# A Mamba block with attention and experts on one core: odd token tiles of the state sum move from VectorE to ScalarE and GpSimd

## What is computed

```python
def step(s, inp):
    d_t, B_t, C_t, u_t = inp
    dA = jnp.exp(d_t[..., None] * A)
    dBu = d_t[..., None] * B_t[:, None, :] * u_t[..., None]
    s = s * dA + dBu
    y = jnp.einsum('bds,bs->bd', s, C_t)     # sum over the 16 states
    return (s, y)
```

## Time and profile before

| what | value |
| --- | --- |
| time, median of 3 runs | 1225.23 us (1220.23 to 1236.71) |
| profiled execution, first to last instruction | 1224.7 us |
| VectorE busy | 922.6 us (75%) |
| TensorE busy | 929.7 us (76%) |
| GpSimd busy | 528.2 us (43%) |
| ScalarE busy | 489.6 us (40%) |
| state sums on VectorE (lines 1100 and 1103) | 256, of which 240 take 167.3 us |
| scan of chunk 0 | 62.8 to 181.4 us |
| ticks 3 to 20 of the scan of chunk 1 | about 258 to 361 us |

### The profile page before, as it was taken

How to read it: one execution, slowest core, us unless ns; L and a number is a source line. 1 busy time by engine, 2 the same in 40 slices (tenths; PEclk the granted TensorE clock), 3 DMA queues, 4 the chain that set the end, 5 groups by cost and what they waited for, 6 DMA issues and landing times.

```text
span 1224.7 us, 13783 instructions
## 1 busy us (share of the span) xinstructions
PE 929.7 (76%) x3960; PEld 700.9 (57%) x3960; DVE 922.6 (75%) x1323; ACT 489.6 (40%) x911; POOL 528.2 (43%) x311
## 2 busy tenths in 40 slices
PE   4845549668689899577689899486789896677996
PEld 2434435256468685165477785165468683554885
DVE  2699996589999966689999965789789965322233
ACT  3534423544246434454345424454245421211442
POOL 1266540453457740533367730544257741001553
PEclk9855558778669999678679899678579997665999
DMA  5100101201023211101023211201023212000331
GB/s 193 36 35 35 52 1 35 70 35 61 18 70 121 77 45 54 70 35 61 18 78 127 73 36 55 85 18 61 18 72 119 86 35 91 21 1 9 117 109 42
DMA packets 38254, 72.61 MB, mean 59 GB/s; under 512 B 3871, under 2 KB 12712, under 8 KB 38174
## 3 DMA queue, kind: packets, MB, share of 16 engines
q1 hardware_dynamic: 38174, 71.65, 17.8%
HBM read 65.14 MB, written 2.30 MB: 55 GB/s over the span
## 4 chain that ended last, share of the span: by engine, by line
PE 45%; DVE 23%; issue 20%; POOL 6%; ACT 3%; DVEq 1%; POOLq 0%; DMA 0%; ACTq 0%; SPq 0%
PE ps L862 11%; DVE hs L1051 7%; PE ps L939 7%; PE ps L718 6%; PE ps L797 5%; POOL dbu L531 4%; DVE yacc L1103 4%; PE ps L836 3%; PE ps L791 2%; PE ps L825 2%; DVE work L1219 2%; PE ps L881 2%; PE ps L776 2%; DVE xn L1014 1%; POOL work L563 1%
## 5 line engine op out<-in xcount | busy, mean ns | idle before, releaser
L531 POOL TENSOR_TENSOR dbu<-v,bbc 128x1024 f32<-128x1024 f32 x128 | 308.9, 2418 | 257.3 <-DVE hs L1051 136.3
L1051 DVE TENSOR_TENSOR_SCAN hs<-ps,carry,dbu 128x512 f32<-128x512 f32 x256 | 313.3, 1266 | 10.1 <-ACT ps L627 8.2
L627 ACT ACTIVATE ps<-delta,neg_a 128x512 f32<-128x512 f32 x256 | 175.7, 692 | 300.5 <-DVE hs L1051 300.4
L718 PE MATMUL ps<-ident,hs 128*128 128x128 f32 x1024 | 189.1, 344 | 116.5 <-DVE yacc L1103 99.5
L718 PEld LDWEIGHTS ps<-ident,hs 128*128 128x128 f32 x1024 | 157.0, 180 | 150.0 <-DVE hs L1051 72.4
L1103 DVE SCALAR_TENSOR_TENSOR yacc<-ps,ctok,yacc 128x512 f32<-128x512 f32 x240 | 167.3, 737 | 1.2 <-PE ps L718 1.0
L555 POOL TENSOR_TENSOR w_lo<-w13s,w_hi 128x512 fp32r<-128x512 f32 x72 | 94.5, 1313 | 145.1 <-ACT w_hi L693 145.1
L939 PE MATMUL ps<-w2s,work 128*128 128x256 f32 x576 | 140.4, 388 | 0.3
L939 PEld LDWEIGHTS ps<-w2s,work 128*128 128x128 f32 x576 | 109.0, 196 | 15.9 <-DVE work L1225 1.5
L1219 DVE SCALAR_TENSOR_TENSOR work<-work 128x512 f32<-128x512 f32 x72 | 82.3, 1143 | 46.5 <-POOL work L563 45.6
L862 PE MATMUL ps<-x_hi,w_hi 128*128 128x512 f32 x288 | 107.9, 457 | 9.4 <-DVE work L1225 9.2
(11 more groups left out here) (159 smaller groups left out, 1243.0 us busy)
## 6 DMA issues: line engine op xcount, KB each, us to landing
w13s<-in_w SPq DMA_DIRECT2D x72, 256.0 KB, 2.9
bbc<-brow_dram SPq DMA_DIRECT2D x32, 512.0 KB, 4.0
w2s<-in_w SPq DMA_DIRECT2D x36, 256.0 KB, 2.7
cbc<-comb_dram SPq DMA_DIRECT2D x32, 256.0 KB, 3.5
work<-work SPq DMA_DIRECT2D x16, 256.0 KB, 2.3
xn<-in_x SPq DMA_DIRECT2D x5, 512.0 KB, 5.3
xt<-in_x SPq DMA_DIRECT2D x4, 512.0 KB, 3.6
rope<-in_rope_q SPq DMA_DIRECT2D x4, 512.0 KB, 4.2
```

The lines of the kernel that those rows point to most:

```text
L531: pool.tensor_tensor(dbu[:, i % DRING, :, :], v[:, 2 * h:2 * h + 2, :], bbc[:, n // 2 % 2, n % 2, :].rearrange("p (o t) -> p o t", o=1) .t ...
L627: act.activation(ps[:, unit % 2, :], delta[:, q, :], ACT.Exp, scale=neg_a[:, q * NS + m:q * NS + m + 1]).then_inc(da_done.sem, 1)
L718: last = pe.transpose(ps[:, bank, t * P:(t + 1) * P], src(t), ident[:, :])
L1051: dve.tensor_tensor_scan(hs[:, m % 2, q, 0:TC], ps[:, unit % 2, :], dbu[:, n % DRING, q % 2, :], carry[:, m, q:q + 1], ALU.mult, ALU.add). ...
```

## The change

For the first nine states (`SHARE = 9`) the odd token tiles are no longer summed by VectorE. ScalarE multiplies PSUM bank 3 by the column of `ctok` (`weigh`), for state 0 straight into `yacc`, for states 1 to 8 into `weighed`, which is the space of `xt`. GpSimd adds `weighed` to `yacc` (`add_weighed`). Even tiles, and all tiles of states 9 to 15, stay with VectorE. A new step, scan2, stands between scan and late: in it ScalarE weighs and then makes the second of its two decays, and GpSimd adds. The semaphore `y_done` is split into four; the transposes of an odd tile of the first nine states wait for `y_mul`, which ScalarE raises. The load of `xt` goes from the start of a body (pre 3) to tick 31 of the scan, behind the last add.

```diff
@@ schedule
-        steps += [("early", t), ("sum", s), ("mid", t), ("scan", s), ("late", t)]
+        steps += [("early", t), ("sum", s), ("mid", t), ("scan", s), ("scan2", s), ("late", t)]
@@ tiles
+        weighed = xt[:, :, :].rearrange("p (a b) n -> p a (b n)", a=2)
@@ sync
-                if kind == "pre" and n == 3:
-                    sp.wait_ge(*res_done.at(j, 0))
+                if kind == "scan" and n == SCAN_TICKS - 4:
+                    sp.wait_ge(*y_add.at(j, 2 * (SHARE - 1)))
                     sp.dma_start(xt[:, :, :], x[bass.ds(j, 1)].rearrange("a t p d -> p (a t) d")
                                  ).then_inc(xt_in.sem, 16)
@@ gpsimd
+                if kind == "scan2" and 5 <= n < 3 + 2 * SHARE:
+                    add_weighed(j, *divmod(n - 3, 2))
...
+            def add_weighed(j, n, half):
+
+                t = 2 * half + 1
+                pool.wait_ge(*y_mul.at(j, 2 * n + half + 1))
+                pool.wait_ge(*y_add.at(j, max(0, 2 * (n - 2) + half + 1)))
+                pool.tensor_tensor(yacc[:, t, :], yacc[:, t, :], weighed[:, half, :], ALU.add
+                                   ).then_inc(y_add.sem, 1)
@@ scalar
-                if kind == "scan":
-                    for unit in range(2 * n + 2 if n else 0, min(2 * n + 4, NS * Q)):
+                if kind == "scan2" and 3 <= n < 3 + 2 * SHARE:
+                    weigh(j, *divmod(n - 3, 2))
+                if kind in ("scan", "scan2"):
+                    ahead = 2 * n + 2 + (kind == "scan2")
+                    for unit in ([ahead] if n or kind == "scan2" else [0, 1, ahead]):
+                        if unit >= NS * Q:
+                            continue
...
+            def weigh(j, n, half):
+
+                t = 2 * half + 1
+                act.wait_ge(*ht_ps.at(j, n * NT + t + 1))
+                if n == 0:
+                    act.wait_ge(*ctok_done.at(j, 1))
+                    act.wait_ge(*xz_ps.at(j, 2 * Q))
+                    act.activation(yacc[:, t, :], ps[:, 3, :], ACT.Copy, scale=ctok[:, t, n:n + 1]).then_inc(y_mul.sem, 1)
+                else:
+                    if n == 1:
+                        act.wait_ge(*res_done.at(j, 0))
+                    else:
+                        act.wait_ge(*y_add.at(j, 2 * (n - 2) + half + 1))
+                    act.activation(weighed[:, half, :], ps[:, 3, :], ACT.Copy, scale=ctok[:, t, n:n + 1]
+                                   ).then_inc(y_mul.sem, 1)
@@ tensor, state_rows
-                    pe.wait_ge(*y_done.at(j, max(0, n * NT + t - 1)))
+                    before = 2 * n + t // 2
+                    if t % 2 == 0:
+                        pe.wait_ge(*y_even.at(j, before))
+                    elif before <= 2 * SHARE:
+                        pe.wait_ge(*y_mul.at(j, before))
+                    else:
+                        pe.wait_ge(*y_odd.at(j, before - 2 * SHARE))
                     transposes(2 + t % 2, lambda q: hs[:, n % 2, q, t * P:(t + 1) * P], Q, ht_ps)
@@ vector, sum_states
                     c = ctok[:, t, n:n + 1]
+                    if t % 2 and n < SHARE:
+                        continue
```

More of the change, by code:

```diff
@@ L43 @@
 HRING = 3
+SHARE = 9
 DRING = 3
@@ L280, in block_kernel @@
         ht_ps = signal("ht_ps", NS * NT)
-        y_done = signal("y_done", NS * NT)
+        y_even = signal("y_even", 2 * NS)
+        y_odd = signal("y_odd", 2 * (NS - SHARE))
+        y_mul = signal("y_mul", 2 * SHARE)
+        y_add = signal("y_add", 2 * (SHARE - 1))
         yt_ps = signal("yt_ps", Q)
@@ L629, in mixer @@
                     m = n // 2 - 1
-                    if n % 2 == 0 and 0 <= m < NS:
+                    if kind == "scan" and n % 2 == 0 and 0 <= m < NS:
                         act.wait_ge(*scan_done.at(j, Q * (m + 1)))
                         act.activation(carry[:, m, :], hs[:, m % 2, :, TC - 1], ACT.Copy).then_inc(carry_done.sem, 1)
+            def weigh(j, n, half):
[12 more added lines that the diff above has]
+                                   ).then_inc(y_mul.sem, 1)
             def convolution_start(j, q):
@@ L781, in mixer @@
                 if kind == "post" and n == 0:
-                    for t in range(NT):
-                        pe.wait_ge(*y_done.at(j, (NS - 1) * NT + t + 1))
+                    pe.wait_ge(*y_even.at(j, 2 * NS))
+                    pe.wait_ge(*y_odd.at(j, 2 * (NS - SHARE)))
                     for q in range(Q):
@@ L1099, in sum_states @@
                         dve.wait_ge(*xz_ps.at(j, 2 * Q))
-                        dve.tensor_scalar(yacc[:, t, :], ps[:, 2 + t % 2, :], c, None, ALU.mult).then_inc(y_done.sem, 1)
-                    else:
-                        dve.wait_ge(*y_done.at(j, (n - 1) * NT + t + 1))
-                        dve.scalar_tensor_tensor(out=yacc[:, t, :], in0=ps[:, 2 + t % 2, :], scalar=c,
-                                                 in1=yacc[:, t, :], op0=ALU.mult, op1=ALU.add).then_inc(y_done.sem, 1)
+                        dve.tensor_scalar(yacc[:, t, :], ps[:, 2, :], c, None, ALU.mult).then_inc(y_even.sem, 1)
+                    elif t % 2 == 0:
+                        dve.wait_ge(*y_even.at(j, (n - 1) * 2 + t // 2 + 1))
+                        dve.scalar_tensor_tensor(out=yacc[:, t, :], in0=ps[:, 2, :], scalar=c,
+                                                 in1=yacc[:, t, :], op0=ALU.mult, op1=ALU.add).then_inc(y_even.sem, 1)
+                    else:
+                        if n == SHARE:
+                            dve.wait_ge(*y_add.at(j, 2 * (SHARE - 2) + t // 2 + 1))
+                        else:
+                            dve.wait_ge(*y_odd.at(j, (n - 1 - SHARE) * 2 + t // 2 + 1))
+                        dve.scalar_tensor_tensor(out=yacc[:, t, :], in0=ps[:, 3, :], scalar=c,
+                                                 in1=yacc[:, t, :], op0=ALU.mult, op1=ALU.add).then_inc(y_odd.sem, 1)
             def row_stats(j, k, src, t, before):
```

## The result

The changed kernel takes 1279.25 us (median of 4 runs, 1277.19 to 1289.54); the kernel before 1225.44 us (4 runs). The ratio is 1.0407, interval 1.0356 to 1.0458: slower by about 4%. The profiled execution has a span of 1279.3 us against 1224.7.

The account below looks back on a forecast made before the run. VectorE was taken to bound chunk 0 only, a loop through four engines chunks 1 to 3. The sum was 1224.7 - 2 + 3 x 17 = 1273.7 us, said as 1273, with a range of 1211 to 1300.

Parts of the forecast that it names:

- The likeliest case of the four: Chunks 1 to 3: transposes held back by the weighing, as walked; 1273 us, range 1251 to 1294, chance 0.64.
- VectorE is not the bound in chunks 1 to 3: Ticks 3 to 20: VectorE's work stands in a loop round four engines, one turn 10.65 us; VectorE binds chunk 0 only.
- The rival of 1178 us: Whole kernel: VectorE is the bound and all 72 sums, 46.8 us, come off; chance 0.09.
- Prices: Added work: 72 weighings on ScalarE at 0.69 us, 64 adds on GpSimd at 1.26 us, moved xt load zero.
- Bank 3 free 2.7 us after the first scan starts: Each changed tick: scan 1.27, exp 0.69, weighing 0.69 and hand-overs pass before the odd transposes can start.
- The walk through chunk 1: Ticks 3 to 20 followed instruction by instruction: first scans shift from -1.3 us at tick 4 to +17 at tick 21.
- 17 us per chunk: Chunks 1 to 3: loss in each from late transposes and what queues behind them; bounds 10 to 23 us.
- the rival of the falling clock: Chunks 1 to 3: longer gaps may lower TensorE's granted clock to 0.6; 1273 + 24 = 1297 us, chance 0.09.
- The collision of top with a dbu: Tick 5, chunk 1: top runs beside a dbu delayed by an add, takes 1.30 us against 0.17 alone, ends with it.
- Chunk 0: Scan without attention beside it: -2 us (0 to -4), with GpSimd at 3.61 us per tick against 3.67.
- GpSimd allows less: 2.35 + 1.26 = 3.61 per tick: Chunk 0: GpSimd's dbu and add limit the tick, against 3.67 before; 1 us over 16 ticks.
- The hidden case, 1211 us: Whole kernel: the wait hides and only short ticks gain, 11.7 us and 2 in chunk 0; with collisions alone, chance 0.18.

Follow-up runs that it names:

- weigh_at_sum: Changed kernel with ScalarE's weighing moved to the step sum, ahead of the exp that waits for the scan: 1243.32 us, ratio 1.0066 to the kernel before.
- weigh_last: Changed kernel with ScalarE's weighing moved behind both exps of the tick: 1354.91 us in one run, 1.097 times the median of the kernel before.
- no_odd: Changed kernel without the odd sums of the first nine states on any engine, nor the wait for bank 3: 1197.95 us, ratio 0.9745 to the kernel before.
- split_only: Kernel before with only the two exps of a tick split as in the change: 1233.02 us, ratio 1.0031.
- no_add: Changed kernel without GpSimd's 64 adds and the waits for them, weighing kept: 1283.89 us, ratio 1.0403 to the kernel before.
- weigh_first: Changed kernel with the weighing in a step of its own, ahead of everything in the tick: 1229.38 us, ratio 1.0008 to the kernel before.
- same_tick: Changed kernel with each tile weighed one tick earlier, behind its own transposes: 1224.65 us, ratio 0.9975 to the kernel before.
- first_chunk: Kernel before with the change in chunk 0 only, one odd tile in two ticks, weighed first; exps split, xt late: 1220.58 us, ratio 0.9845; again 1221.6, 0.9855.

## Why the prediction was right

**The sum.** 1273 was predicted, 1279.25 measured, the span 1279.3 against 1273.7: 54.6 us more instead of 49. The likeliest case of the four happened, for its reason: weigh_at_sum takes five sixths of the loss away and weigh_last more than doubles it, by the place of one instruction.

**VectorE is not the bound in chunks 1 to 3: right.** no_odd is the direct measure. Without the 72 sums the kernel gains 31 us and not 46.8; chunk 0 gives the whole of its part, the three others about half of theirs in the profile, and less at a like clock. (The shares were read a little high: 95.92 of 107.90 us is 89%, so VectorE was busy for 89 to 95%.) The rival of 1178 us is out of reach even for a kernel that does not do the work at all. The Trainium skill, "Perfetto Trace Analysis", section "Optimizing Scalar/DVE Operations", says that moving work off a saturated DVE may make sense. Here VectorE is saturated in chunk 0 alone, and the ratios are 1.0407 as it was done, 1.0008 with the weighing first and 0.9845 with chunk 0 alone.

**Prices: nearly right.** The weighing took 0.67 us (0.69 taken), the add 1.285 (1.26). Moving the load of xt was not tried alone; at the same clock no stage shows a cost or a gain from it.

**Bank 3 free 2.7 us after the first scan starts: right.** In tick 4 the scan starts at 264.09, the weighing ends at 266.80 and the transposes start at 266.86, after 3.27 us of waiting.

**The walk through chunk 1: right in its steps.** Where the earlier trace rows has the transposes of normalised x 0.06 us behind VectorE's pieces, and 0.14 us behind the start of the scan, tick 16 of the changed kernel has:

```profile
353.93 2.44 DVE L1093 TENSOR_TENSOR_SCAN hs<-ps,carry,dbu 128x512 f32<-128x512 f32 x2
...
355.96 0.67 ACT L667 ACTIVATE xt<-ps,ctok 128x512 f32<-128x512 f32 x1
...
356.68 1.11 PE L754 MATMUL ps<-ident,hs 128*128 128x128 f32 x4 [5.36 <-ACT xt L667]
...
357.59 1.91 PE L754 MATMUL ps<-ident,x 128*128 128x128 f32 x8
```

They start 3.66 us behind the scan (3.8 predicted). The shift of a tick's first scan, in us, each chunk from its own tick 2:

| tick | predicted | chunk 1 | chunk 2 | chunk 3 |
|---|---|---|---|---|
| 4 | -1.3 | -0.2 | 0.0 | -1.0 |
| 6 | +1.6 | +3.7 | +1.2 | +2.6 |
| 8 | +3.1 | +4.9 | +3.4 | +4.8 |
| 10 | +7.0 | +8.6 | +9.6 | +11.4 |
| 12 | +8.8 | +11.0 | +12.3 | +14.1 |
| 15 | +11.4 | +15.4 | +13.7 | +13.1 |
| 18 | +15.6 | +21.8 | +17.2 | +13.7 |
| 21 | +17 | +23.3 | +18.9 | +15.1 |
| 31 | +17 | +23.3 | +19.0 | +15.8 |

**The mis-sized term: 17 us per chunk, measured 19.4 on average.** Most of the excess is in chunk 1, where the granted clock was 0.63 against 0.72 before, and TensorE was busy for 85.93 us instead of 76.97: the rival of the falling clock, in one chunk of three. Beside stretches of the old program at about the same clock, ticks 3 to 20 are longer by 14.4 us in chunk 1 (124.47 at 0.63, split_only 110.08 at 0.64) and by 14.2 in chunk 3 (120.40 against 106.25, both at 0.70), to which the ticks around them add 1 to 2. So at a like clock the loss is 15 to 16 us per chunk, close to the walk's 17, and the rest of the 19.4 goes with a lower clock than in the one profile of before. Whether the waits themselves lower the clock was not tested.

**The collision of top with a dbu: right in kind, too large, without effect.** The walk let top end with the dbu, 0.9 us after the maximum. In tick 5 it did end with the dbu (276.40 and 276.36), but it began later and so took only 0.68 us, some 0.5 more than alone; and no_add, which has no adds, loses as much. The walk came near the measured shift of tick 6 with this term because another one was off: tick 4 was to begin 1.3 us earlier and began 0.2 earlier in chunk 1.

**Chunk 0: the size right (-1.4 for -2), the cause wrong.** "GpSimd allows less: 2.35 + 1.26 = 3.61 per tick" was the step that failed. The timeline of the changed kernel there:

```profile
128.09 2.42 POOL L538 TENSOR_TENSOR dbu<-v,bbc 128x1024 f32<-128x1024 f32 x1
129.01 0.67 ACT L667 ACTIVATE xt<-ps,ctok 128x512 f32<-128x512 f32 x1
...
129.82 1.94 PE L754 MATMUL ps<-ident,hs 128*128 128x128 f32 x8 [0.99 <-ACT xt L667]
130.40 1.34 POOL L547 TENSOR_TENSOR yacc<-yacc,xt 128x512 f32<-128x512 f32 x1
131.12 2.46 DVE L1093 TENSOR_TENSOR_SCAN hs<-ps,carry,dbu 128x512 f32<-128x512 f32 x2 [0.95 <-PE ps L754]
131.63 2.42 POOL L538 TENSOR_TENSOR dbu<-v,bbc 128x1024 f32<-128x1024 f32 x1
```

GpSimd runs without a gap, a dbu every 3.54 us (128.09 to 131.63; 3.61 predicted); but the scan waits for the transposes, not for GpSimd, and no_add keeps the 4.04 us of the odd tick. The slot of hs sets it: 3.02 + 4.04 = 7.06 us a pair, where 6.84 was worked out, because the hand-overs of an odd tick took 0.4 us and not 0.2. Two ticks of GpSimd come to 7.08, so the two bounds are nearly equal, and the near hit on the size is luck. Not foreseen was that 1 us is given back at tick 20, when VectorE takes up the odd tiles.

**The hidden case, 1211 us: too good.** It left the moved work at no price once the wait hides. weigh_first has the wait out of the way and stands at 1.0008; the 0.67 us on ScalarE are on the same loop. Had the change been written that way, the price of a moved instruction on its new engine would have been the missing term.

## What to carry to other kernels

Work moved to another in-order engine takes the release of its buffer with it: look at what stands ahead of it in that engine's order (here an exp that waits for a scan) and at what is queued behind whoever waits for the buffer (here all of a tick's late work on TensorE). Put the release ahead of the waits; but if both engines lie on one loop, as in chunks 1 to 3, the move gains nothing even then. Move work only in the stages where the receiving engine is off the path, here chunk 0. More than that engine can take brings little there: all 18 odd tiles, weighed early, gained 6.5 to 7.3 us (weigh_first, same_tick), and 13 of them 6.7.

## What the runs showed of the hardware

Ticks 3 to 20 of the old program, the same work each time, took 100.24 us at a mean granted clock of 0.77 and 109.53 us at 0.67 in one and the same execution (first_chunk, chunks 3 and 2), 100.93 at 0.77 in the kernel before and 110.08 at 0.64 in split_only. So a stage can differ by 9% between chunks or profiles though the kernels' times agree. I had not expected that a chunk's length was so loose; it is why the readings here rest on ratios of many runs, on stretches at a like clock, and on waits that change several times over. What decides which clock a chunk gets is not shown.

GpSimd's operations in chunk 0 of the changed kernel, which follow each other without a gap, grew a little longer on the way: dbu from 2.35 to 2.42 us and add from 1.27 to 1.34. Why is not shown.
